# Third norm's transposes behind the next round's first scores, and a feed-forward eviction behind the step's last exponentials, in a four-layer transformer decoder

## The reference

```
x = norm1(x + out1(attention(q1 x, k1 x, v1 x, mask)))          # 16 heads of 16
x = norm2(x + out2(attention(q2 x, k2 context, v2 context)))
x = norm3(x + W2 relu(W1 x + b1) + b2)                           # 1024 hidden units
```

## Time and profile before

| | |
|---|---|
| median of 3 runs | 3507.88 us (3506.46 to 3513.25) |
| the profiled execution | 3517.44 us, of which span 3515.7 us |
| TensorE busy, share of the span | 88% |
| ScalarE, VectorE, GpSimd | 56%, 56%, 47% |
| mean granted TensorE clock | 0.956 of full |

### The profile page before, as it was taken

The page is one execution under the profiler, slowest core; times in us unless marked ns, Lnnn a source line. Parts: engine busy times, 40 slices in busy tenths (PEclk is TensorE's granted clock), DMA queues, the critical chain, the costliest instruction groups (busy, mean ns, idle before and its releaser), DMA issues. The chain is left out here.

```text
span 3515.7 us, 81973 instructions
## 1 busy us (share of the span) xinstructions
PE 3087.0 (88%) x28275; PEld 2679.8 (76%) x28400; DVE 1985.9 (56%) x4082; ACT 1961.5 (56%) x7922; POOL 1648.8 (47%) x2002
## 2 busy tenths in 40 slices
PE   7999997799999999537999999999999999848886
PEld 5999997488888889536888888788888888745564
DVE  2455554344444444335777777777777777635665
ACT  2444443233344444226777777777777777626775
POOL 1233333114444444512566666666666666652445
PEclk8999998899999999868999999999999999979998
DMA  2222221401111110032221222233111111122321
GB/s 100 64 69 66 78 72 37 147 28 37 52 51 45 51 50 19 36 110 73 82 70 59 67 68 70 86 90 112 58 56 58 59 54 56 36 74 65 102 85 56
DMA packets 218094, 232.77 MB, mean 66 GB/s; under 512 B 41920, under 2 KB 183232, under 8 KB 215360
## 3 DMA queue, kind: packets, MB, share of 16 engines
q1 hardware_dynamic: 217920, 230.49, 20.8%
HBM read 148.57 MB, written 65.01 MB: 61 GB/s over the span
## 5 line engine op out<-in xcount | busy, mean ns | idle before, releaser
L1719 ACT ACTIVATE middle_stage<-middle_psum,middle_neg_max 128x128 f32<-128x128 f32 x2048 | 727.7, 386 | 358.5 <-DVE middle_neg_max L1699 358.2
L1719 ACT ACTIVATION_READ_ACCUMULATOR middle_stage<-middle_psum,middle_neg_max 128x1 f32 x2048 | 462.2, 226 | 0.0
L1699 DVE TENSOR_REDUCE middle_neg_max<-middle_psum 128x4 f32<-128x512 f32 x512 | 337.4, 681 | 63.0 <-PE middle_psum L1662 62.9
L1673 PE MATMUL middle_psum<-middle_eye,middle_stage 128*128 128x128 f32 x2048 | 322.1, 280 | 19.2 <-DVE middle_p_turned_odd L1705 9.4
L1673 PEld LDWEIGHTS middle_psum<-middle_eye,middle_stage 128*128 128x128 f32 x2048 | 232.5, 142 | 71.0 <-issue 46.5
L1621 POOL COPY middle_inverse_row<-middle_inverse 128x128 f32<-128x128 f32 x256 | 68.6, 297 | 381.6 <-DVE middle_inverse L1588 348.5
L1786 POOL TENSOR_SCALAR middle_n_z<-middle_n_z,middle_n_moments,middle_n_rstd 128x256 f32<-128x256 f32 x192 | 234.7, 1229 | 20.3 <-POOL middle_n_rstd L1781 20.3
L536 POOL TENSOR_TENSOR cross_ff_hidden_lo<-cross_ff_relu,cross_ff_hidden_hi 128x256 fp32r<-128x256 f32 x128 | 101.2, 792 | 284.9 <-DVE cross_ff_hidden_hi L531 284.9
L1901 POOL TENSOR_TENSOR middle_ff_hidden_lo<-middle_ff_relu,middle_ff_hidden_hi 128x256 fp32r<-128x256 f32 x256 | 184.2, 740 | 52.8 <-DVE middle_ff_hidden_hi L1895 52.8
L97 PE MATMUL middle_psum<-middle_n_yt_hi,middle_w_lo 128*128 128x256 f32 x640 | 194.7, 304 | 14.4 <-DVE middle_n_yt_lo L1833 9.7
L1705 DVE COPY middle_p_turned_odd<-middle_psum 128x512 f32<-128x512 f32 x256 | 174.8, 683 | 34.4 <-PE middle_psum L1673 34.3
(11 more groups left out here) (341 smaller groups left out, 10880.7 us busy)
## 6 DMA issues: line engine op xcount, KB each, us to landing
middle_stage<-middle_a_k SPq DMA_DIRECT2D x1024, 16.0 KB, 1.8
middle_xt_hi<-x_hi SPq DMA_DIRECT2D x32, 256.0 KB, 2.7
middle_xt_lo<-x_lo SPq DMA_DIRECT2D x32, 256.0 KB, 3.0
middle_ct_hi<-context_hi SPq DMA_DIRECT2D x32, 256.0 KB, 2.9
middle_ct_lo<-context_lo SPq DMA_DIRECT2D x32, 256.0 KB, 3.2
middle_x_rows<-x_rows SPq DMA_DIRECT2D x32, 256.0 KB, 2.8
middle_mask_flags<-flags SPq DMA_DIRECT2D x128, 64.0 KB, 1.9
x_rows<-middle_n_z SPq DMA_DIRECT2D x32, 256.0 KB, 2.2
```

Of the source, the lines that this page charges most:

```text
L1673: ins = pe.transpose(banks.psum[:, TURN_BANK, x * SEQ:(x + 1) * SEQ], self.sh.p_wide[:, 4 * b + t, x, :], self.sh.eye[:])
L1699: dve.tensor_reduce(self.sh.neg_max[:, 4 * b + t, :], psum[:, SCORE_BANKS[t], :].rearrange("p (x k) -> p x k", x=4), AX_X, ALU.max, negate ...
L1719: ins = act.activation(self.sh.p_wide[:, 4 * b + t, x, :], psum[:, SCORE_BANKS[t], x * SEQ:(x + 1) * SEQ], ACT.Exp, bias=self.sh.neg_max[: ...
```

## The change

Three calls move, and nothing is added or taken away. On TensorE, `norm3.pe` goes from the end of y1 to the next round's x0, behind `turn(x0[1], 0)`; and the feed-forward output product `out(3, 4)` goes from behind `turn(x0[1], 2)` to just behind `norm3.pe`, ahead of hidden pair 6. On ScalarE, the relu of hidden pair 4 goes in y1 from ahead of the last group of exponentials, `exp(y1_next, 3)`, to behind it; and norm3's cast, `norm3.act_hi`, goes in x0 from right behind `norm3.act` to behind `spread(x0)`.

```diff
@@ ScalarE, x0
                 if ok(-4):
                     norm3.act(act, Back(r, 4), psum)
-                    norm3.act_hi(act, Back(r, 4), stored)
                 exp(x0_next, 0)
                 if ok(-3):
                     ff.act_relu(act, Back(r, 3), psum, 6)
                 exp(x0_next, 1)
                 spread(x0)
+                if ok(-4):
+                    norm3.act_hi(act, Back(r, 4), stored)
                 if ok(-1):
                     proj2.act_q(act, Back(r, 1), psum)
@@ ScalarE, y1
                 exp(y1_next, 2)
+                exp(y1_next, 3)
                 if ok(-2):
                     ff.act_relu(act, Back(r, 2), psum, 4)
-                exp(y1_next, 3)
@@ TensorE, x0
                 scores(x0[2])
                 turn(x0[1], 0)
+                if ok(-4):
+                    norm3.pe(pe, Back(r, 4), banks)
+                out(3, 4)
                 if ok(-3):
                     ff.pe_hidden(pe, Back(r, 3), banks, 6)
                 turn(x0[1], 1)
...
                 turn(x0[1], 2)
-                out(3, 4)
                 if stream.is_next(Back(r, 1)):
                     layer.pe_swapped(pe, "v2")
@@ TensorE, y1
                 turn(y1[1], 3)
                 out(2, 3)
-                if ok(-3):
-                    norm3.pe(pe, Back(r, 3), banks)
```

## The result

The changed kernel takes 3546.95 us (median of 4 runs, 3543.34 to 3548.72) against 3508.28 us before (4 runs): the ratio is 1.0103, with a 95% interval of 1.0088 to 1.0118. It is slower. Five rounds more beside the experiments gave 3543.14 us and a ratio of 1.0092 (1.0075 to 1.0108).

A forecast was written before the change was run, and what follows sets the result against it. TensorE's issue and waits bound the middle stage. x0 +0.46 +0.52 +0.77 and y1 -0.71 give +1.04 us a round, over 28 rounds +29 us: 3537 us; own range 3528 to 3545, 8 in 10 3518 to 3554.

The forecast's parts named there:

- (D): ScalarE late, holding up q's eviction or the next scores: 0.3 to 0.8 us more a round, 3545 to 3560 us; 12%.
- Edit 1: End of y1: relu of pair 4 behind the last exponentials frees score banks earlier, seam gains 0.71 us a round.
- Edit 2: norm3's transposes behind turn(0): free in y1, they add 0.46 us of issue to x0 each round.
- The wait it makes: In x0, hidden pair 6 waits for ScalarE's eviction of norm3 from the shared bank: +0.52 us a round.
- Edit 3: In x0, out(3,4) taken from behind turn(2) leaves q's eviction partly uncovered, so v waits: +0.77 us a round.
- Edit 4: In x0, norm3's cast behind spread fits before q's eviction by 0.2 us and costs nothing.
- The signs: Trace: y1 near 11.4, x0 near 13.5 us, new waits about 0.5 (hidden pairs) and 0.75 us (v), PE busy time unchanged.
- (E): TensorE's clock falls to half for one 3.4 us stretch a round: 48 us more, 3585 us; 3%.
- (A): Faster: both evictions stay hidden and the seam's gain is kept, -0.25 us a round, 3501 us; 5%.
- (B): Effects cancel: only one new wait appears, or both at about half; +1 us in all, within 0.2%; 6%.
- (C): Only one new wait in x0: 3522 us without hidden 6's, 3515 us without v's; 7%.
- (F): Seam stays because PE comes late, not the banks; its gain is lost, +1.75 us a round, 3557 us; 2%.

The follow-up runs named there:

- edit 1 alone: Kernel before with only the relu of hidden pair 4 moved behind the last exponentials in y1: 3526.78 us, ratio 1.0044.
- edit 3 undone: Changed kernel with out(3,4) put back behind turn(2), the rest as changed: 3544.82 us, ratio to before 1.0092.
- Edit 3 alone: Kernel before with only out(3,4) moved from behind turn(2) to behind turn(0): 3533.13 us, ratio 1.0056.
- edit 2 alone: Kernel before with only norm3's transposes moved from the end of y1 to behind turn(0) of the next x0: 3563.07 us, ratio 1.0148.

## Why the prediction was right, point by point

The forecast was 3537 us with a range of 3518 to 3554; the time is 3546.95. The mechanism was right in what decides the time: a gain at the seam, and a new wait at each of the two evictions that lost their cover. The sum came out small: +1.04 us a round against a measured (56.0 - 21.0) / 28 = +1.25. The forecast's own range, 3528 to 3545, misses 3546.95 and holds the 3543.14 of the second measurement; that the wide range holds both is in part luck, as its upper end came from rival (D), whose cause did not occur.

- *Edit 1.* The 0.71 us at the seam measured 0.75. The run with edit 1 alone showed that it needs edit 2: without it the same edit costs 0.57 us.
- *Edit 2.* The issue of the transposes was put at 0.46 us. In x0 turn(0) takes 0.50 instead of 0.42 before them and they take 0.35 (2165.31, 2165.81, 2166.16), 0.43 together.
- *The wait it makes* was put at 0.52 us. out(3,4) is done 0.79 us after 2166.16, at 2166.95, and hidden pair 6 starts at 2167.60: 0.65 us in the hardware loops. In the rounds that are written out it is 0.08 us less (hidden pair 6 starts at 3.65 us of the step and not at 3.73). Of the error of 0.13 us, then, 0.08 belong to the loop; the rows that I had added the chain from are of round 14, which is written out.
- *Edit 3* was put at 0.77 us, as a price beside norm3's wait. The run with edit 3 undone shows that the two are one price: without this edit norm3's wait would be longer by about the same. turn(2) ends its issue at 2172.35 + 0.36 = 2172.71, v starts at 2173.44: 0.73 us. What I left out is that the groups themselves can take longer. v's twelve matmuls take 1.54 us to the next turn (2173.44 to 2174.98 in TensorE's timeline) against 1.49 before; with edit 3 undone, where v doesn't wait, they take 1.48 again. Hidden pair 6 takes 1.51 us against 1.45, but 1.50 in the third layer before, without a wait, so that part isn't the wait's doing. Together some 0.1 us a round in the second layer, 2 to 3 us in all.
- *Edit 4* at nothing: right, by the run that undoes it. ScalarE is idle for 0.22 us between the cast and q's eviction, where the forecast had 0.2.
- *What the sum did not have.* In three rounds at the switch of layers out(3,4) waits for GpSimd. I had taken GpSimd's low half of unit 4 as covered by 0.7 us in each round; where a weight swap stands behind the relu, it is not. ScalarE's swap, VectorE's and only then the split, from the timelines of the four engines in the changed kernel:

```profile
2359.76 0.67 ACT L2131 CAST middle_w_hi<-middle_w_hi 128x512 fp32r<-128x512 f32 x1
...
2360.46 0.69 DVE L2136 TENSOR_TENSOR middle_w_lo<-middle_w_lo,middle_w_hi 128x512 fp32r<-128x512 f32 x1 [1.82 <-ACT middle_w_hi L2131]
...
2361.23 0.42 DVE L1895 CAST middle_ff_hidden_hi<-middle_ff_relu 128x256 fp32r<-128x256 f32 x2
...
2362.00 1.41 POOL L1901 TENSOR_TENSOR middle_ff_hidden_lo<-middle_ff_relu,middle_ff_hidden_hi 128x256 fp32r<-128x256 f32 x2
...
2362.77 0.38 PE L97 MATMUL middle_psum<-middle_w_hi,middle_ff_hidden_lo 128*128 128x256 f32 x1 [0.90 <-POOL middle_ff_hidden_lo L1901]
```

  out(3,4) waits 0.90 us, hidden pair 6 then hardly at all, and x0 is 14.1 to 14.2 us in these rounds. Edit 3 alone has the same (x0 +1.5 to +1.65 us in them), and with edit 3 undone these rounds are 13.6 to 13.8 us without such a wait. So the wait comes from out(3,4)'s new place. That the swap is what makes the low half late is read off the timelines; no run took the swap away. It is worth 1.3 us for the three rounds together, above their neighbours. And in most rounds of the third layer's loop x0 is 13.9 to 14.1 us, where the scores take 0.15 to 0.33 us longer to follow the mask matmuls. It adds some 2 us in all. It shows in each of the seven traces with the order scores, turn(0), norm3's transposes in x0, though not in every round of them, and in none of the others (nor with turn(0) ahead of the scores). Its cause was not tried and stays open.
- *Together.* Over the 28 rounds the longer wait behind norm3 adds 3 us to the forecast, the longer groups 2 to 3, the rounds at the switch 1.3 and the scores of the third layer 2, while the terms put too high take 3 away: 5 to 6 us, where the steps exceed the forecast by 5.
- *The signs.* The waits and the lengths of x0 and y1 came as named, but v's wait is in the list with 0.50 us (13.9 in 28) and not 0.75, since the list counts from the end of turn(2). TensorE's busy time was not unchanged: it grew by 9 us over the rounds.
- *The clock* (E). 1.00 over the whole stage, with seven waits a round in place of five. The rule of the Trainium skill, page "TensorE: Matmul & The Clock Gate", section "A second HAM failure mode: psum-queue depth-cycling", that I weighed against the change has no part here: by that rule the waits between groups could have made the clock swing; the trace does not agree.
- *The rivals.* (A) and (B) needed an eviction hidden or an elastic x0; edit 3 alone, at +0.56% with 0.39% as its lower bound, rules that out. (C), one wait only, is wrong, though the run with edit 3 undone shows that (C)'s "without v's" is reachable only by making hidden pair 6's wait longer by the same. (D) as I put it, ScalarE late by the cast, is wrong; the time is at its edge for other reasons. (F) is wrong: y1 is 11.33 us with edit 1 and 12.07 without it (edit 2 alone), where the seam's wait is twice as long.

The sum over the steps gives +34 us for the 28 rounds. The medians differ by 38.7 us (first) and 31.9 us (again), and +34 us, a ratio of 1.0097, lies within both intervals.

## What to carry to other kernels

Where several products share one PSUM bank, list for each what stands between it and the next user of the bank, and compare that cover with the eviction. In this kernel, moving a user of the bank cost its whole eviction at its new place unless it found cover there, and cover taken from elsewhere was missed there: two placements of the same 0.79 us block gave the same time. To use a wait at a seam, move into it the work that claims neither of the resources being waited for: the four softmax transposes that need only their own bank gave 0.4% here with two lines moved.

## What the runs showed of the hardware that was not expected

v's twelve matmuls take 0.05 to 0.06 us longer when they start behind a wait (1.54 against 1.48 and 1.49 us). One ScalarE instruction of 512 columns in place of two of 256 saves 0.24 us in norm3's eviction (0.78 against 1.02 us) and 0.15 us in q's (0.69 against 0.84), and the waits behind them shrink by as much. And profiled executions of nearly the same code differ outside the changed rounds: the middle stage's first scores came at 1539.5 us in the trace of before, 1.8 us earlier in that of the changed kernel and about 8 us earlier when it ran again, which is why the 34 us were taken from the steps and not from two spans.
